# Attention on one core: ScalarE instead of GpSimd multiplies head 0's probabilities with the inverse of their sum

## What is computed

```python
scores = q @ k^T * SCALE + q . rel_k[dist]          # 8 sequences, 16 heads, 512 x 512
threshold = top_k(scores, 32)[..., -1:]
scores = where(scores < threshold, -inf, scores)
attn = softmax(scores)
v_curr = v
for i in range(3):
    a_v = attn @ v_curr                              # the first one also adds attn . rel_v[dist]
    v_curr = a_v
    res += sigmoid(alphas_raw)[i] * v_curr
out = res @ Wout.T + bout
```

## Time and profile before

| | |
|---|---|
| median of three runs | 3022.24 us (3021.09 to 3027.37) |
| the profiled execution's own time | 3027.0 us |
| its span, first to last instruction | 3025.3 us, mean granted clock 0.912 |
| VectorE (DVE) busy | 2678.7 us, 89% |
| TensorE (PE) busy | 2549.6 us, 84% |
| GpSimd (POOL) busy | 2245.4 us, 74% |
| ScalarE (ACT) busy | 2070.2 us, 68% |
| attention: first search of VectorE to the last mixing work | about 66 to 2350 us |

### The profile page before, as it was taken

One profiled execution on the slowest core, in us unless ns is written; L12 is line 12 of the kernel. 1 busy time (PEld: TensorE's weight loads), 2 busy tenths in 40 slices (PEclk: granted clock), 3 DMA queues, 4 the chain that ended last, 5 costly groups with the idle time before them and its releaser, 6 DMA issues. The chain is left out here.

```text
span 3025.3 us, 61812 instructions
## 1 busy us (share of the span) xinstructions
PE 2549.6 (84%) x16480; PEld 1500.3 (50%) x16480; DVE 2678.7 (89%) x6575; ACT 2070.2 (68%) x6271; POOL 2245.4 (74%) x2796
## 2 busy tenths in 40 slices
PE   4688889888888888888988888888887586998857
PEld 2444544444444444454444444444444345777743
DVE  4999999999999999999999999999995474766646
ACT  2688888888888888888888888888886152222214
POOL 1799999999999999999999999999997151222105
PEclk7799999999999999999999999999999596767759
DMA  3344444444444444444444444444442000000001
GB/s 105 105 121 121 121 119 123 122 119 122 120 123 119 122 120 122 120 119 126 118 120 122 120 121 121 119 121 123 120 118 75 8 22 15 8 4 4 0 8 50
DMA packets 373488, 286.47 MB, mean 95 GB/s; under 512 B 30174, under 2 KB 369192, under 8 KB 373160
## 3 DMA queue, kind: packets, MB, share of 16 engines
q1 hardware_dynamic: 371012, 280.38, 32.8%
q10 hardware_dynamic: 2148, 2.33, 0.3%
HBM read 139.48 MB, written 136.58 MB: 91 GB/s over the span
## 5 line engine op out<-in xcount | busy, mean ns | idle before, releaser
L869 DVE MAX8 top<-work 128x8 f32<-128x512 f32 x1536 | 986.2, 689 | 0.0
L879 DVE MATCH_REPLACE8 work<-top,work 128x512 f32<-128x512 f32 x1024 | 689.7, 686 | 0.0
L955 POOL TENSOR_TENSOR scores<-scores,cut 128x512 f32<-128x512 f32 x512 | 645.1, 1283 | 0.0
L554 PE MATMUL bank<-probs_t,u 128*64 128x512 f32 x2048 | 467.8, 599 | 11.5 <-ACT u L766 1.4
L946 POOL TENSOR_SCALAR cut<-scores,minus_max_and_least 128x512 f32<-128x512 f32 x512 | 355.7, 695 | 63.1 <-issue 39.5
L818 ACT ACTIVATE probs_of_tile<-scores,minus_max_and_least 128x512 f32<-128x512 f32 x512 | 376.2, 763 | 21.0 <-POOL scores L955 20.2
L965 POOL TENSOR_SCALAR probs_of_tile<-probs_of_tile,inverse 128x512 f32<-128x512 f32 x512 | 350.5, 696 | 25.5
L879 DVE MATCH_REPLACE8 work<-top,scores 128x512 f32<-128x512 f32 x512 | 344.8, 686 | 0.0
L866 DVE MAX8 top<-scores 128x8 f32<-128x512 f32 x512 | 327.5, 686 | 10.8 <-ACT scores L759 10.8
L951 POOL TENSOR_SCALAR cut<-cut 128x512 f32<-128x512 f32 x512 | 306.7, 615 | 21.6
L759 ACT ACTIVATE scores<-bank 128x512 f32<-128x512 f32 x512 | 273.9, 585 | 55.7 <-PE bank L606 55.3
(11 more groups left out here) (252 smaller groups left out, 5033.9 us busy)
## 6 DMA issues: line engine op xcount, KB each, us to landing
probs_scratch<-probs_of_tile SPq DMA_DIRECT2D x256, 256.0 KB, 2.5
band<-probs_scratch SPq DMA_DIRECT2D x256, 256.0 KB, 3.1
rel_scratch<-rel SPq DMA_DIRECT2D x256, 254.0 KB, 3.1
relj<-rel_scratch SPq DMA_DIRECT2D x256, 128.0 KB, 2.4
relj<-rel_scratch SPq DMA_DIRECT2D x512, 64.0 KB, 2.5
experts_xs<-stream_normed_t SPq DMA_DIRECT2D x16, 256.0 KB, 2.3
stream<-in_L_attn_a_x SPq DMA_DIRECT2D x4, 512.0 KB
mixer_xs<-stream_normed_t SPq DMA_DIRECT2D x8, 256.0 KB, 2.3
```

What stands on the lines that cost most here:

```text
L554: last = nc.tensor.matmul(U[HEADS[h], lo:hi], lhs, pt[mpar][:, h, jt, lo:hi], start=(jt == 0 and lo == 0), stop=(jt == NT - 1 and step > 0))
L869: nc.vector.max(top[q][:, h, 8 * r:8 * r + 8], work[:, h, :]).then_inc(s.next_tops, 1)
L879: nc.vector.match_replace(out=work[:, h, :], in_to_replace=top[q][:, h, 8 * r:8 * r + 8], in_values=sc[Tc][:, h, :] if r == 0 else work[:, ...
L955: nc.gpsimd.tensor_tensor(sc[Tc][:, h, :], sc[Tc][:, h, :], cut[:, h, :], ALU.add).then_inc(s.masked, 1)
```

## The change

ScalarE multiplies head 0's exponentials with their inverse, as an activation `Copy` with a per-partition scale; GpSimd keeps head 1. Head 0 gets a semaphore of its own, `first_probs`. The semaphore `probs` now counts one a tile instead of two. Who waited for `probs` (SyncE's store, TensorE's transposes, VectorE's inverse) now waits for both.

```diff
 # SyncE, ahead of the store of the band (L491)
-                    c0, c1 = known(sp, 2 * n + 2, 16 * (it * 2 + Td // 2))
+                    c0, c1 = known(sp, n + 1, 16 * (it * 2 + Td // 2))
                     sp.wait_ge(s.probs, c0)
+                    sp.wait_ge(s.first_probs, c0)
...
 # TensorE, ahead of the transposes (L653)
-                    pe.wait_ge(s.probs, 2 * n + 2)
+                    pe.wait_ge(s.first_probs, n + 1)
+                    pe.wait_ge(s.probs, n + 1)
...
 # ScalarE, between the band's copy (L805) and the exponentials (L818)
+                y = z.back(5)
+                if y:
+                    it, Ty, n = y
+                    act.wait_ge(s.inverse, n + 1)
+                    row = t.prob[Ty][:, 0, HALF:HALF + N]
+                    nc.scalar.activation(row, row, ACT.Copy, scale=inv[Ty][:, 0:1]).then_inc(s.first_probs, 1)
...
 # VectorE, ahead of the inverse (L850)
-                            dve.wait_ge(s.probs, 2 * n - 6)
+                            dve.wait_ge(s.probs, n - 3)
+                            dve.wait_ge(s.first_probs, n - 3)
...
 # GpSimd (L965)
-                    for h in range(2):
-                        row = t.prob[Ty][:, h, HALF:HALF + N]
-                        nc.gpsimd.tensor_scalar(row, row, inv[Ty][:, h:h + 1], 1.0,
-                                                ALU.mult, ALU.mult).then_inc(s.probs, 1)
+                    row = t.prob[Ty][:, 1, HALF:HALF + N]
+                    nc.gpsimd.tensor_scalar(row, row, inv[Ty][:, 1:2], 1.0, ALU.mult, ALU.mult).then_inc(s.probs, 1)
```

More of the change, by code:

```diff
@@ L414, in attention @@
     s.probs = sem("att_probs")
+    s.first_probs = sem("att_first_probs")
     s.probs_turned = sem("att_probs_turned")
```

## The result

The changed kernel takes 3069.6 us (median of 4 runs, 3061.78 to 3072.48) against 3023.95 (4 runs of the kernel before on the same chip, 3021.09 to 3027.37): a ratio of 1.0142, 95% interval 1.0123 to 1.0161. That is slower, as forecast. The forecast was 3077 us, and its range holds the time.

What follows compares the result with a forecast made beforehand. VectorE, at 8.77 us a slot, was taken to bound the kernel. Old disturbances 18.7, clock falls 40.0, less the lead 3.8, gave +55 us on 3022.2, so 3077 us; range 3028 to 3112.

Steps and rivals of the forecast that it cites:

- The bound and the relief: Attention: VectorE's 8.77 us a slot sets the time; GpSimd's saved 0.68 us a slot gains nothing.
- Rival (d): VectorE in attention: less GpSimd traffic makes it faster; 0.1 us a slot would give 2996 us; chance 0.04.
- The cost of the new instruction: ScalarE, each slot: the added multiplication takes 0.57 us, with ends of 0.53 and 0.71.
- Hidden in three slots: ScalarE, slots 0, 1 and 3: the instruction hides in band DMA waits of 1.01, 0.89 and 1.19 us.
- The chain in slot 2: ScalarE and TensorE, slot 2: the 8.70 us chain grows 0.57 us, making ScalarE's iteration 35.08, equal to VectorE's.
- Rival (c): Slot 2: the new instruction is hidden there too, so no change, 3022 us; chance 0.11.
- The falls of the clock: TensorE, slot 2: longer idle time lowers the clock in two of five iterations, 1.64 us each, 40.0 us.
- Rival (b): TensorE, slot 2: the clock falls in every iteration, +115 us, 3137 us; chance 0.08.
- (a): TensorE's clock stays up; ScalarE's loop bounds but only old disturbances are paid, +15 us, 3037 us; chance 0.17.
- The other disturbances: ScalarE's loop, 61 iterations from tile 12 on: delays already in the kernel before recur and are paid, 18.7 us.
- The lead: ScalarE's scores copy ahead of VectorE at tile 12: 3.8 us can be lost before VectorE waits, taken off.
- Behind attention: Stages after attention's last search: no added time in the sum, zero.

Runs made afterwards that it cites:

- e5: Kernel before, with head 0's multiplication on GpSimd left out and put nowhere else: 3022.86 us, ratio 0.9992.
- e1: Changed kernel, with ScalarE's new instruction moved behind the query copy in slot 2 only: 3032.78 us, ratio 1.0018.
- e2: Changed kernel, but ScalarE multiplies head 0 only for the tile met in slot 2, GpSimd does the rest: 3053.46 us, ratio 1.011.
- e3: Changed kernel, but ScalarE multiplies head 0 only in slots 0, 1 and 3; GpSimd does both heads in slot 2: 3030.19 us, ratio 1.0016.
- e4: Changed kernel plus four unread matmuls on TensorE in the idle time before slot 2's values product: 3039.35 us, ratio 1.0042.
- e6: Changed kernel, with slot 2's query copy moved ahead of the new instruction and the exponentials: 3030.09 us, ratio 1.0016.
- e7: e6 with the inverse of the row sums moved from VectorE to GpSimd and ScalarE's multiplication behind the exponentials: 3014.26 us, ratio 0.9963.

## Why the prediction was right, and where its sizes were off

- **The bound and the relief.** VectorE's 8.77 us a slot set the time, and GpSimd's relief was worth nothing: right, shown by e5. Rival (d) is out with it.
- **The cost of the new instruction.** I took 0.57 us from the key copies; it is 0.61, inside the ends given (0.53 to 0.71). The estimate of 0.61 from the Trainium skill (ScalarE: Activation LUTs, What ACT_TABLE_LOAD costs) agrees with this trace's 0.61. A nearer row than the key copies was at hand: the exponentials L818 read SBUF as the new instruction does, where the key copies read PSUM, and one of them held ScalarE from 1220.52 to 1221.13, 0.61 us:

```profile
1221.13 0.25 ACT L818 ACTIVATION_READ_ACCUMULATOR probs_of_tile<-scores,minus_max_and_least 128x1 f32 x1
```

- **Hidden in three slots.** Right, 25.62 and 25.63 us for the three; but the cover was more than the band waits I named. Only slot 1 pays out of its band wait (0.33 us at 1134.60, where 0.89 stood). In slots 3 and 0 the instruction fills ScalarE's wait for the mixing product: 63.9 us in 114 waits of L721 before, no such row after. I had not looked at that wait.
- **The chain in slot 2.** Right: 9.31 us for a forecast of 9.27, idle time before the values 1.80 for 1.76, and e1, e2 and e3 show that of the four places this one brings the loss in the search stage. Rival (c) is out: TensorE and the copy behind it did move.
- **The falls of the clock.** This is the term that was mis-sized. "Two in five", 24 of 61 at 1.64 us, made 40.0; 17 of 59 at 1.52 made 25.9. Eight idle times of the kernel before were too few for a share. (In the working of the range, five in eight give +77, not +78.) That falls make up most of the loss is shown by e4, where they were taken away with the delay left in. Rival (b), a fall in every iteration, is out. So is (a) as a whole, since the clock did fall; but its +15 for what is left without falls was near: e4's search stage has +9.3, its median +14.1.
- **The rule on short pauses.** Seventeen falls behind idle times like the 1.80 us of 1142.61 speak against the rule in the Trainium skill (TensorE: Matmul & The Clock Gate, Why this matters for your kernels) by which pauses that short pass without a drop.
- **The other disturbances.** I took 18.7 us over from the kernel before. The 59 iterations took 2105.34 us; 59 x (34.51 + 0.61) are 2072.1, and of the 33.3 left, 25.9 are falls. So some 7 us remain, not 18.7. My reading is that part of what ScalarE lost before was lost while it had time to lose, and I counted it as if it must recur; no run separates this.
- **The lead.** I had it last a dozen iterations at most. After the start VectorE waited again at 146.03 us, for tile 9: the lead was used up before the point from which I had counted it as 3.8 us, so that little of it was saved.
- **Behind attention.** I took zero. The stages behind the last search took 6.5 us longer, in unchanged code. That this belongs to the change is not shown; see below.

The measured terms: falls 25.9, other disturbances 7.4, and 59 x (35.12 - 35.08) = 2.4 for the larger price make 35.7 of the search stage's 38.5; the other 2.8 lie outside these 59 iterations. The two large errors of the sum point the same way (14 us too many for falls, 11 for other disturbances), and the lead that I took off and the 6.5 us behind attention that I had not counted hide a part of that: 55 forecast, 45.5 measured. So the total came nearer than its terms, which is luck.

**Left open:** what decides whether the clock falls behind an idle time of 1.80 us, since it did and did not with the same idle time. It does not look like chance: from 932 to 1291 us it fell in every second iteration, as these rows with the two at 1110.97 (0.61) and 1147.41 (2.11) show in part, but no run tests what sets that order.

```profile
1075.97 1.09 ACT L762 ACTIVATE scores<-bank 128x512 f32<-128x512 f32 x2 [2.22 <-PE bank L608]
...
1182.43 1.09 ACT L762 ACTIVATE scores<-bank 128x512 f32<-128x512 f32 x2 [0.61 <-PE bank L608]
```

Also open is the 0.2% of e1, e3 and e6. In their profiled executions all that follows the end of GpSimd's last addition of attention to the stream took 674.6 to 678.3 us, 672.0 before and 678.5 after the change; but it was 662.7 in e5 and 668.6 in e4, so that single executions do not tell it apart. The granted clock from 2353 to 3010 us was 0.70 in e1, e3 and e6, 0.71 before and 0.73 in e5, which points to the clock behind attention; but e7 took 676.2 us there at 0.72, and no run tests it.

## What to carry to other kernels

An engine that is busy for 68% can still have no time to give: follow the loop that runs through it and the engines that wait for it, and price new work slot by slot along that loop. Put added work behind the instruction for which another engine waits, not ahead of it; here that one move takes away the whole loss of the search stage, and all but 0.2% of the time. And price a delay ahead of a run of matmuls by what TensorE's clock does behind the longer idle time too: here 0.6 us of delay cost 1.5 us more in 17 of 59 iterations.

## What I had not expected of the hardware

- The same idle time, 1.80 us before the same matmuls, was followed by a granted clock of 1.00 at 1107 us and of 0.63 at 1143 us. Four matmuls whose result nobody reads, in place of that idle time, took away every fall at that place.
- A `pow` on GpSimd of two columns takes 0.72 us by its row, as long as its multiplication of 512 columns by a scalar, 0.69 (1107.79 and 1108.69 in e7). Yet the exchange pays, because the reciprocal that it replaces, on two columns as well, is worth 0.06 us a slot on the engine that sets the pace.
